# Two channels per TensorE product in the first layer's protein sums, with the gated pairs stored as two planes of 32 channels

## The reference

```
pp = _ln(protein_pair, ln_w)                       # 256 x 256 x 128
pp = sigmoid(pp @ gw2) * (pp @ w2 + b2)            # 256 x 256 x 64: the gated pairs
block1 = einsum('bikc,bkjc->bijc', pp, ab1)        # for each channel c: (i x k) times (k x j)
block2 = einsum('bikc,bjkc->bijc', ab2, cp)
out = g * (_ln(block1 + block2, lnc_w) @ ws + bs) * z_mask
```

## Time and profile before

| | |
|---|---|
| median of three runs | 2763.47 us (2761.99 to 2766.56) |
| the profiled execution, first to last instruction | 2758.7 us |
| PE busy / PEld busy / DVE busy / ACT busy in it | 2063.0 / 1644.6 / 1483.6 / 1194.8 us |
| first layer's `protein_sums` in it | about 281 to 723 us |
| second layer's `protein_sums` in it | about 2040 to 2152 us |

### The profile page before, as it was taken

How to read it: one execution, slowest core, us unless ns; L and a number is a source line. 1 busy time by engine, 2 the same in 40 slices (tenths; PEclk the granted TensorE clock), 3 DMA queues, 4 the chain that set the end, 5 groups by cost and what they waited for, 6 DMA issues and landing times. The chain is left out here.

```text
span 2758.7 us, 52709 instructions
## 1 busy us (share of the span) xinstructions
PE 2063.0 (75%) x13026; PEld 1644.6 (60%) x13027; DVE 1483.6 (54%) x6345; ACT 1194.8 (43%) x3197; POOL 1194.5 (43%) x1319
## 2 busy tenths in 40 slices
PE   6978789889787120003999999947789767999996
PEld 2437576676566110002888888834489446998995
DVE  5765857658496531112333333328821696776666
ACT  2325747548155000001555555524410265776665
POOL 2434323224297177774555555547720473001221
PEclk9989899999866555556999999969989678999998
DMA  4001313213351211112222222125375220000003
GB/s 127 0 16 47 107 54 99 69 54 106 143 199 60 71 52 51 53 52 64 70 72 70 71 73 70 60 86 168 118 153 122 63 60 7 0 0 1 0 0 123
DMA packets 248917, 193.96 MB, mean 70 GB/s; under 512 B 94904, under 2 KB 210934, under 8 KB 248830
## 3 DMA queue, kind: packets, MB, share of 16 engines
q1 hardware_dynamic: 231422, 159.09, 19.8%
q0 software_dynamic: 17408, 33.87, 3.4%
HBM read 123.09 MB, written 71.86 MB: 71 GB/s over the span
## 5 line engine op out<-in xcount | busy, mean ns | idle before, releaser
L1526 POOL DMA_INDIRECT choices<-ab_tiles x288 | 287.5, 998 | 255.1 <-ACT ab_tiles L1560 184.3
L357 POOL TENSOR_TENSOR small<-small 128x4 f32<-128x4 f32 x192 | 197.3, 1028 | 351.1 <-DVE small L350 351.1
L1435 POOL DMA_INDIRECT sorted_tokens<-work x256 | 247.3, 966 | 121.3 <-issue 81.1
L1597 PE MATMUL banks<-w,hidden 128*128 128x128 f32 x2304 | 276.4, 279 | 0.0
L1574 PE MATMUL banks<-ident,ab_tiles 128*128 128x128 f32 x288 | 44.3, 277 | 308.7 <-DMA ab_tiles<-sorted_tokens 308.7
L1597 PEld LDWEIGHTS banks<-w,hidden 128*128 128x128 f32 x2304 | 262.7, 192 | 16.3 <-ACT hidden L1551 16.1
L1659 PE MATMUL banks<-small 128*128 128x128 f32 x1536 | 239.8, 293 | 6.5 <-DVE small L1714 3.7
L374 ACT ACTIVATE small<-small 128x128 f32<-128x128 f32 x384 | 161.6, 483 | 146.5 <-DVE small L362 145.7
L386 PE MATMUL banks<-ident,small 128*128 128x128 f32 x640 | 124.1, 313 | 133.6 <-ACT small L374 109.7
L1574 PEld LDWEIGHTS banks<-ident,ab_tiles 128*128 128x128 f32 x288 | 34.5, 144 | 309.3 <-DMA ab_tiles<-sorted_tokens 309.1
L1652 PE MATMUL banks<-ab_tiles,small 128*128 (+1 forms) x1536 | 214.8, 277 | 5.0 <-DMA small<-L_ffn_V_o 5.0
(11 more groups left out here) (217 smaller groups left out, 5007.1 us busy)
## 6 DMA issues: line engine op xcount, KB each, us to landing
small<-L_conv_protein_pair SPq DMA_DIRECT2D x128, 256.0 KB
sorted_tokens<-work SPq DMA_DIRECT2D x32, 585.0 KB
ab_tiles<-sorted_tokens SPq DMA_DIRECT2D x72, 260.0 KB, 2.8
work_again<-choices SPq DMA_DIRECT2D x32, 512.0 KB, 3.9
work_again<-L_conv_protein_pair SPq DMA_DIRECT2D x32, 512.0 KB, 6.1
x_tiles<-x SPq DMA_DIRECT2D x32, 256.0 KB, 3.6
work<-x SPq DMA_DIRECT2D x32, 256.0 KB, 3.1
after_mixture<-x_tiles SPq DMA_DIRECT2D x32, 256.0 KB, 2.2
```

What stands on the lines that cost most here:

```text
L357: self.scaled.done(pool.tensor_tensor(self.r[:, u, :], self.var[:, u, :], self.mhalf, ALU.pow))
L1435: pool.indirect_dma_start(out=self.sorted, out_offset=bass.IndirectOffsetOnAxis(ap=where[:, u, t, k:k + 1], axis=0), in_=rows[:, u, t, k, ...
L1526: pool.indirect_dma_start(out=self.out, out_offset=bass.IndirectOffsetOnAxis(ap=rows[:, u, t, E + 1:ROW].bitcast(U32), axis=0), in_=y[:, u ...
L1597: last = pe.matmul(out[:, t * P:(t + 1) * P], hidden[:, u % 2, h, t * P:(t + 1) * P], w2[:, u % 2, h * P:(h + 1) * P], start=False, stop=h ...
```

## The change

In the first layer only, the gated pairs are stored in another order and two channels go into one product.

The tile `pp` is seen as `ppq`, with dimensions (k, h, kc, q, i, 32 channels): channel c and channel c + 32 stand in two planes q = 0 and q = 1. `squash` and `gate` write 4 rows x 2 planes x 32 channels in place of 4 rows x 64 channels. A product takes for its weights the 128 columns (q, i) of one c in 0..31, which lie 32 floats (128 bytes) apart, and as its moving operand the 128 columns (q, j) of channels c and c + 32, which lie 128 floats apart within a q. Its 128 x 128 result holds channel c in the upper left quarter and channel c + 32 in the lower right one; the other two quarters are not used. A bank now holds four such results, and DVE adds it in two instructions of 64 partitions x 64 x 4 elements, one for each q. The second layer takes the path that it took before.

The core of the diff (in the new file the product stands at line 849 and the addition at line 806; the lines before the change are 906 and 864):

```diff
     def squash(self, act, dest, n, u):
-        self.squashed.done(act.activation(dest, self.out_bank(u)[:, :, 0, :], ACT.Sigmoid))
+        self.squashed.done(act.activation(dest, self.halves(dest, self.out_bank(u)[:, :, 0, :]), ACT.Sigmoid))
+    def halves(self, dest, out):
+        return out if len(dest.shape) == 3 else out.rearrange("p g (q c) -> p g q c", q=2)
...
+            ppq = pp.rearrange("p h k i c -> p (h k i c)").rearrange("p (h k q i c) -> p h k q i c", h=2, k=2, q=2, i=C)
...
-                                stream.gate(dve, pp[:, 1 - h, kc, bass.ds(i, G), :], base + m, u)
+                                stream.gate(dve, ppq[:, 1 - h, kc, :, bass.ds(i, G), :].rearrange("p q i c -> p i q c"), base + m, u)
...
+                                for q in range(2):
+                                    at = q * (C // 2) + c8 * 4
+                                    sums = chip.ab[rows, bass.ds(ic * NC_, NC_), 1, at:at + 4]
+                                    own = chip.banks[q * C:(q + 1) * C, 4 + c8 % 4, :].rearrange(
+                                        "p (c q j) -> p q j c", q=2, j=NC_)[:, q, :, :]
+                                    last = dve.tensor_tensor(sums, own, sums, ALU.add)
...
-                            for cc in range(8):
+                            if not raw_pairs:
+                                for cc in range(4):
+                                    c = c8 * 4 + cc
+                                    for kc in range(ICS):
+                                        last = pe.matmul(
+                                            chip.banks[:, 4 + c8 % 4, cc * P:(cc + 1) * P],
+                                            ppq[:, 1 - h, kc, :, :, c].rearrange("p q i -> p (q i)"),
+                                            chip.ab[:, kc * NC_:(kc + 1) * NC_, 0, :].rearrange(
+                                                "p j (q c) -> p q j c", q=2)[:, :, :, c],
+                                            start=kc == 0, stop=kc == ICS - 1)
+                            for cc in range(8 if raw_pairs else 0):
```

More of the change, by code:

```diff
@@ L642, in squash @@
         self.projected.ready(act, n)
-        self.squashed.done(act.activation(dest, self.out_bank(u)[:, :, 0, :], ACT.Sigmoid))
+        self.squashed.done(act.activation(dest, self.halves(dest, self.out_bank(u)[:, :, 0, :]), ACT.Sigmoid))
+    def halves(self, dest, out):
+        return out if len(dest.shape) == 3 else out.rearrange("p g (q c) -> p g q c", q=2)
     def gate(self, dve, dest, n, u):
         self.squashed.ready(dve, n)
-        self.gated.done(dve.tensor_tensor(dest, dest, self.out_bank(u)[:, :, 1, :], ALU.mult))
+        self.gated.done(dve.tensor_tensor(dest, dest, self.halves(dest, self.out_bank(u)[:, :, 1, :]), ALU.mult))
 ROWS = 16
@@ L861, in _ @@
                             n = (ic * 2 + h) * 8 + c8
-                            sums = chip.ab[rows, bass.ds(ic * NC_, NC_), 1, c8 * 8:(c8 + 1) * 8]
                             blocked.ready(dve, n)
-                            summed.done(dve.tensor_tensor(
-                                sums, chip.banks[rows, 4 + c8 % 4, :].rearrange("p (c j) -> p j c", c=8), sums, ALU.add))
+                            if raw_pairs:
+                                sums = chip.ab[rows, bass.ds(ic * NC_, NC_), 1, c8 * 8:(c8 + 1) * 8]
+                                last = dve.tensor_tensor(
+                                    sums, chip.banks[rows, 4 + c8 % 4, :].rearrange("p (c j) -> p j c", c=8), sums, ALU.add)
+                            else:
+                                for q in range(2):
[4 more added lines that the diff above has]
+                                    last = dve.tensor_tensor(sums, own, sums, ALU.add)
+                            summed.done(last)
             @block.scalar
@@ L878, in squash @@
                             kc, i = where(m, u, h)
-                            stream.squash(act, pp[:, 1 - h, kc, bass.ds(i, G), :], base + m, u)
+                            stream.squash(act, ppq[:, 1 - h, kc, :, bass.ds(i, G), :].rearrange("p q i c -> p i q c"), base + m, u)
                         engine_loop(act, per_chunk, 4, [(lambda m, u: stream.apply_act(act, base + m, u), 0),
```

## The result

| | median | range | ratio to before |
|---|---|---|---|
| before | 2762.73 us (4 runs) | 2759.57 to 2766.56 | |
| with the change | 2793.39 us (4 runs) | 2792.29 to 2795.74 | 1.0105, 95% interval 1.0082 to 1.0128 |

The change makes the kernel 30.7 us slower. I had forecast 2763.0 us with 2726 to 2770 as the range. The profiled executions have spans of 2758.7 and 2790.9 us.

What follows compares the result with a forecast made beforehand. The prediction took TensorE's four product blocks to be on the path: -1.0 us from products and +0.5 us from additions gave -0.5 us, so span 2758.2 us and median 2763.0 us, range 2726 to 2770.

Steps and rivals of the forecast that it cites:

- upper bound of the products: Product blocks: a new 128-column record costs at most twice line 906's 110.3 ns, 220.6 ns; 219 was taken.
- term of the four blocks: Four product blocks: each 28.16 us against 28.41, together -1.0 us.
- The blocks are on the path: Four product blocks, 113.6 us: TensorE works alone, so a microsecond taken from them comes off the whole.
- A record costs by its columns, since stride costs: Line 906's products: a strided column costs two contiguous ones (line 1380), so doubled columns give 217 to 220.6 ns.
- fixed part of 3.5 ns: Line 906's record: the part not growing with columns, 110.3 - 106.8 ns, giving 217 ns for the new record.
- The planes gain nothing by 128 bytes in place of 256: Product weights: 128 bytes apart still puts no two reads in one 16-byte line, so no gain.
- Additions: DVE's bank additions: the pair takes 0.81 us where one took 0.69; only each block's eighth counts, +0.5 us.
- Squash and gate: 128 instructions each on ACT and DVE: writing runs of 32 channels costs nothing; gate 416, squash 376 ns as before.
- Rival B: Products: strided load grows less than in proportion, record 147 to about 200 ns, 2726 to 2748 us; chance 0.20.
- Rival C: Products: a record costs by its number, 110.3 to 112 ns, total 2709 us; chance 0.07.
- Rival D: Projection parts: gate writing runs of 32 costs 0.27 us more each, +35 us, 2798 us; chance 0.08.
- a record over 230 ns: Product blocks: main case among the small mishaps left over; chance 0.05 for all of these.

Runs made afterwards that it cites:

- experiments 2: Changed kernel keeping its order of pairs in memory, but one channel in each product and one addition per bank, as before the change: 2795.88 us, ratio 1.0117.
- experiment 4: Changed kernel with only the first layer's gated pairs moved by 64 bytes in memory: 2760.77 us, ratio 0.9984.
- experiment 6: Kernel before the change with only the first layer's gated pairs moved by 128 bytes: 2803.61 us, ratio 1.0138.
- experiment 9: Kernel of experiment 8, with squash and gate running the four rows innermost, so they write 16-byte runs: 2715.36 us, ratio 0.9815.
- experiment 1: The first grid: changed kernel, first layer's product blocks replaced by test banks with different weight and moving strides; 112 ns a record with both contiguous, 288 with the change's operands.
- experiment 7: Changed kernel with gated pairs stored channel by channel, so a product's 128 weights are contiguous; moving operand still strided: 2789.56 us, ratio 1.0083.
- experiment 5: Test banks replacing the first layer's block1, weights and moving columns at varied distances and strides; 64-column records took 110 to 114 ns apart, 143 when colliding.
- S64: Label in the test banks for product weights 64 floats (256 bytes) between columns, as in the kernel before the change; moving operand alone, 128 columns: 221 ns with the pair.
- bank 865: Test bank of experiment 5: 64-column products, weights 256 bytes apart, moving channel shifted by 32, which brings both together: 143 ns a record.
- experiment 8: Kernel of experiment 7, with the first layer's token products also stored channel by channel, so both operands are contiguous: 2743.81 us, ratio 0.9918.

## Why the prediction was wrong

The step that failed is the upper bound of the products. I wrote that strict proportion, 220.6 ns a record, was the upper end of what I would consider, and that I need not know which half leads. The record cost 278 ns. The term of the four blocks, -1.0 us, was +29.4. Point by point:

- *The blocks are on the path.* Right: what four blocks lost or gained came out in the total within 2 us in the result and in experiments 2 and 4, and less closely in experiment 6 (35 us of the blocks, 42 in the total) and experiment 9 (55 and 46), where other stages moved too.
- *A record costs by its columns, since stride costs.* Right where the two sides don't meet: 217 to 221 ns at 128 strided columns on both sides (experiment 1), 218 in the whole kernel (experiment 4), which came out at 2760.8 us against my 2763.0. The moving side costs the same as the load, and they run side by side. Doubling line 906's price was sound. The support that I took from line 1380, half of its 213.6 ns, was luck: contiguous records follow the clock and strided ones don't (last section), so a strided column costs about as much as two contiguous ones only at clock 1.00, and the fixed part of 3.5 ns that I drew from the two is shown by no run.
- *The planes gain nothing by 128 bytes in place of 256.* I weighed the stride by itself and found it neutral. It is neutral by itself. It was not in combination: weights 128 bytes apart pass through both halves of the 256-byte period, so half of them fall into the moving column's 16 bytes; weights 256 bytes apart stayed 128 bytes off it all the time. In the change's product the moving planes, too, are 128 bytes apart. No row of the kernel before shows a collision, so its place could not be read from there. But the earlier trace rows showed one placement only, and I carried its price to another placement without a word on that. It was a size taken from a row that differed in something I held to be without effect.
- *Additions.* Predicted 0.81 us for the pair and +0.5 us in all. The pair takes 0.85, the pause behind a block grew by 0.18, 0.7 us in all. Reading 64 partitions and writing 64 others costs nothing that shows: all 64 additions of line 806, with and without it, take 416 to 428 ns.
- *Squash and gate.* Right: 416 and 376 ns, as before. Runs of 32 floats are long enough; single floats are not (experiment 7).
- *Rival B* had no case: no pair of 32-bit operands with 128 columns, one of them with a step of 16 bytes or more, came out under 212 ns. *Rival C* fell likewise, but its number is reachable, 112 ns, once both operands are contiguous. *Rival D* fell for this change, although it named nearly the time that came (2798): gate and squash stayed at 416 and 376 ns.
- *The chances.* Slower had 0.11, and only 0.05 stood for a record over 230 ns. I took for a bound what was only a proportion, and gave a change that moves data in memory no rival on where it comes to stand.
- The Trainium skill, "Advanced Engine Details and Errata", section "SBUF Cachelines", holds in the grid: a step of 8 bytes, two reads to a line, costs 117 to 120 ns, one of 16 bytes or more 213 to 240. The Trainium skill, "TensorE: Matmul & The Clock Gate", section "Step-by-step: what each phase is for", says that loading the next weights doesn't take read bandwidth from the running product. Here the trace doesn't agree, and the measurement decides: 110 ns became 143 and 218 became 278 by the place of the operands alone, so the two reads do meet. At what point in the chip they meet is open.

## What to carry to other kernels

Price a product by the access pattern of both operands: before packing more into a product, bring its columns together, which here halved a record (218 to 112 ns) where packing two channels with a stride gave nothing. If a product of strided operands is slower than either side alone, compare the two start addresses in their low eight bits; a shift of 64 or 128 bytes is a short test. Where data must be written in another order, let the innermost loop of the writing instruction make runs of 16 bytes, as here (686 and 572 ns became 415 and 376).

## What the runs showed of the hardware

- **A collision of the two read streams.** Weights and moving columns that fall into the same 16 bytes of a 256-byte period cost 33 ns a record at 64 columns (110 to 143) and 60 ns at 128 (218 to 278; the 287 and 288 of the grids hold the long first record). Half of the reads colliding costs nearly as much as all of them, 140 and 147 ns from start to start in mid-bank at 64 columns. Only 32-bit operands were tried.
- **Strided records don't follow TensorE's clock.** The stretches of experiment 5 below are, in order, weights 384 bytes off (bank 861), S64 shifted by 36 (869) and by 16 (871), with the length, busy (x records), clock, DMA. At clock 1.00, 0.50 and 0.86 they cost 110, 112 and 111 ns. Colliding ones don't either: 144 ns at 1.00 in bank 865 of experiment 5, and 144 for 64-column records at 0.50 in experiment 6. Contiguous ones do: 112 ns at 1.00 and 213 at 0.50 in experiment 8 (the version of 2743.81 us). So the 110.3 ns of the earlier trace rows were no count of array cycles, although for each column they had come out as 2.07 times one.

```profile
371.85:373.60 1.75, 1.75 (x18) 1.00 0.00 0
...
380.30:382.00 1.70, 1.70 (x18) 0.50 0.00 0
382.10:383.80 1.70, 1.70 (x18) 0.86 0.00 0
```

- **The granted clock fell inside busy blocks.** In the shifted kernel of experiment 6, TensorE came out of a projection part, paused for 1.01 us, was busy without a gap from then on, and stood at 0.50 (1.2 GHz) over the stretch below. For these records it cost nothing. In the changed kernel all four blocks had 0.95; in the kernel before three had 1.00, one 0.94, and all took 28.41 us. Why it falls there I have not tested.

```profile
368.00:372.00 4.00, 4.00 (x30) 0.50 0.00 0
```
